# A state-space scan in two chunks of 256 tokens in place of four of 128, inside a fused Mamba-2 and LoRA kernel

## The reference

```python
A_cs = jnp.cumsum(A_dt, axis=-1)                      # within a chunk
Lmat = jnp.exp(segsum(A_dt))                          # exp(cs[l] - cs[s]), l >= s
M = einsum('bclhn,bcshn->bclsh', Cc, Bc) * Lmat       # C B^T times the decays
Y_diag = einsum('bclsh,bcshp->bclhp', M, X)           # inside a chunk
states = einsum('bclhn,bclhp->bchpn', Bc * exp(A_cs[-1] - A_cs), X)
new_states = einsum('bzjh,bzhpn->bjhpn', decay_chunk, states)   # recurrence over the chunks
Y_off = einsum('bclhn,bchpn->bclhp', Cc, prev_states) * exp(A_cs)
y = Y_diag + Y_off + D * hs
xg = y * silu(gate)                                   # then an RMS norm per group and out_proj
```

## Time and profile before

| | |
|---|---|
| median of 3 runs | 1766.87 us (1766.46 to 1768.51) |
| profiled execution | 1765.04 us, of which span 1763.3 us |
| busy: PE, DVE, ACT, POOL | 94%, 77%, 67%, 62% |
| share of the chain that ended last: PE, DVE, ACT | 72%, 17%, 5% |
| rows of the main loop | first L561 of batch 0 at 132 us, last L561 at 865 us; batch 1: 1009 and 1742 us |

### The profile page before, as it was taken

One profiled execution on the slowest core, in us unless ns is written; L12 is line 12 of the kernel. 1 busy time (PEld: TensorE's weight loads), 2 busy tenths in 40 slices (PEclk: granted clock), 3 DMA queues, 4 the chain that ended last, 5 costly groups with the idle time before them and its releaser, 6 DMA issues.

```text
span 1763.3 us, 28877 instructions
## 1 busy us (share of the span) xinstructions
PE 1666.0 (94%) x9694; PEld 1368.8 (78%) x9694; DVE 1354.8 (77%) x2398; ACT 1187.2 (67%) x2436; POOL 1084.6 (62%) x1358
## 2 busy tenths in 40 slices
PE   5889999999999999999868899999999999999997
PEld 4677878787878888788656778787878787887875
DVE  4877787877778787877668677878787878778785
ACT  2357777777777777777414577777777777777773
POOL 4236667666766667666543267666766676667764
PEclk9999999999999999999979899999999999999998
DMA  4144344334433344333132343344434443344431
GB/s 144 36 126 126 130 138 138 121 123 136 138 127 124 129 138 138 120 127 120 34 105 61 116 138 128 114 138 138 134 119 127 138 138 125 118 137 138 135 105 47
DMA packets 82434, 212.03 MB, mean 120 GB/s; under 512 B 11056, under 2 KB 27696, under 8 KB 82032
## 3 DMA queue, kind: packets, MB, share of 16 engines
q1 hardware_dynamic: 82288, 210.20, 36.8%
HBM read 207.01 MB, written 3.15 MB: 119 GB/s over the span
## 4 chain that ended last, share of the span: by engine, by line
PE 72%; DVE 17%; ACT 5%; issue 4%; DMA 1%; POOL 0%; SPq 0%; DVEq 0%; POOLq 0%; ACTq 0%
PE bh L454 20%; PE bg L454 17%; PE bo L593 15%; PE by L569 6%; DVE cv L618 5%; PE bt L561 4%; PE bt L580 4%; PE bt L600 2%; DVE acc L636 2%; ACT cv L258 2%; DVE mt L827 1%; DVE S L643 1%; DVE by L819 1%; PE bo L540 1%; PE bt L454 1%
## 5 line engine op out<-in xcount | busy, mean ns | idle before, releaser
L391 POOL TENSOR_TENSOR wl<-raw,wh 128x256 fp32r<-128x256 f32 x576 | 527.6, 947 | 146.1 <-ACT wh L254 146.1
L438 POOL TENSOR_TENSOR wol<-raw_o,woh 128x256 fp32r<-128x256 f32 x256 | 184.6, 743 | 483.0 <-ACT woh L358 483.0
L618 DVE SCALAR_TENSOR_TENSOR cv<-bh,par_sb,cv 128x511 f32<-128x511 f32 (+2 forms) x408 | 304.6, 747 | 191.0 <-ACT cv L258 185.8
L267 ACT ACTIVATE mt<-cs_row,cs_tok 128x128 f32<-128x128 f32 x1024 | 324.4, 389 | 0.0
L593 PE MATMUL bo<-woh,xh 128*128 128x512 f32 x512 | 212.7, 415 | 2.8 <-POOL xl L426 2.8
L593 PE MATMUL bo<-woh,xl 128*128 128x512 f32 x512 | 201.7, 394 | 0.0
L593 PE MATMUL bo<-wol,xh 128*128 128x512 f32 x512 | 199.9, 390 | 0.0
L325 ACT ACTIVATE xh<-xg 128x512 fp32r<-128x512 f32 x128 | 81.0, 633 | 166.1 <-DVE xg L823 166.1
L263 ACT ACTIVATE bh<-cv 128x512 f32<-128x512 f32 x136 | 81.8, 601 | 160.5 <-DVE cv L618 160.5
L426 POOL TENSOR_TENSOR xl<-xg,xh 128x256 fp32r<-128x256 f32 x256 | 182.6, 734 | 9.9 <-ACT xh L325 9.9
L811 DVE SCALAR_TENSOR_TENSOR sg<-tg,bg 128x512 f32<-128x512 f32 x128 | 87.9, 687 | 124.9 <-ACT tg L354 124.9
(11 more groups left out here) (168 smaller groups left out, 3354.5 us busy)
## 6 DMA issues: line engine op xcount, KB each, us to landing
raw<-in_w_step SPq DMA_DIRECT2D x128, 512.0 KB, 3.6
cs_row<-cs_rows SPq DMA_DIRECT2D x128, 512.0 KB, 4.3
raw_o<-in_w_out SPq DMA_DIRECT2D x128, 256.0 KB, 2.7
ec_row<-ec_rows SPq DMA_DIRECT2D x256, 96.0 KB, 3.7
raw<-in_w_bc SPq DMA_DIRECT2D x16, 512.0 KB, 4.1
acc<-in_x SPq DMA_DIRECT2D x2, 1024.0 KB, 8.6
mt<-in_w_ffn SPq DMA_DIRECT2D x2, 1024.0 KB, 7.6
out_dram<-acc SPq DMA_DIRECT2D x2, 1024.0 KB, 4.9
```

Of the source, the lines that this page charges most:

```text
L267: e = act.activation(mt[:, m % 2, h, chunk(j)], cs_row[:, m % 2, h, chunk(j)], ACT.Relu, bias=cs_tok[:, b, j, 2 * m + h:2 * m + h + 1], sc ...
L391: e = pool.tensor_tensor(wl[:, n % 2, part], raw[:, n % 2, part], wh[:, n % 2, part].bitcast(F32), ALU.subtract)
L438: e = pool.tensor_tensor(wol[:, 1 - u, part], raw_o[:, 1 - u, part], woh[:, 1 - u, part].bitcast(F32), ALU.subtract)
L618: dve.scalar_tensor_tensor(out=cv[:, u, k:], in0=src[:, 0:L - k], scalar=par_sb[:, un % UNITS, TAPS - 1 - k:TAPS - k], in1=cv[:, u, k:], o ...
```

## The change

The scan's chunk becomes 256 tokens (`CL`), so a batch has two chunks (`NC`). Of each chunk's 256x256 triangle three blocks of 128x128 are kept, as a row of 256 columns and one of 128 (`TRI` = 384 columns), for both chunks 768 in place of 512. Part by part, in a round of the main loop:

- line 267: the rows of blocks 0 and 2 get 256 columns, those of blocks 1 and 3 stay 128; `mt` has 1536 columns in place of 1024, so have the exp and the product with `gt`;
- state products: two, added up in PSUM, in place of three; the products inside a chunk: 8 as before, 4 of them with 256 columns; the carried product: one of 256 columns in place of three of 128, which waits for ScalarE's copy of the state and no longer for VectorE's recurrence;
- `next_state` (4 VectorE instructions) is gone; `xd`, `yo` and `by` plus `yo` have 256 columns in place of 384; each of the two `ec_row` DMAs brings 256 columns in place of 384.

In the group loop the B-C product has 256, 128, 256, 128 columns and two PSUM banks; the mask is applied in two instructions of 384 columns in place of one of 512; B is transposed for two blocks in place of three; the tables are made in rounds 4, 5 and 6, with one buffer in place of one per batch, and `cd_bc` is gone. In the prologue the cumulative sum is two instructions of 256 columns, the decay to the chunk's end one of 256 in place of three of 128. The core of the diff:

```diff
-NS = NJ - 1
+CL = 2 * P
+NC = L // CL
+TRI = CL + P
+        def span(j):
+            return slice(P * j, CL * (j // 2) + CL)
+        def tri(j):
+            return slice(TRI * (j // 2) + CL * (j % 2), TRI * (j // 2) + (CL if j % 2 == 0 else TRI))
...
                 for j in range(NJ):
-                    e = act.activation(mt[:, m % 2, h, chunk(j)], cs_row[:, m % 2, h, chunk(j)], ACT.Relu,
-                                       bias=cs_tok[:, b, j, 2 * m + h:2 * m + h + 1], scale=-1.0)
+                    e = act.activation(mt[:, m % 2, h, tri(j)], cs_row[:, m % 2, h, span(j)], ACT.Relu,
+                                       bias=cs_tok[:, j, 2 * m + h:2 * m + h + 1], scale=-1.0)
...
                         for j in range(NJ):
-                            mm = pe.matmul(bo[2][:, chunk(j)], h2[:, u, chunk(j)], ct[:, g - 1, chunk(j)],
-                                           start=True, stop=True)
+                            mm = pe.matmul(bo[2 + j // 2][:, CL * (j % 2):CL * (j % 2) + (P if j % 2 else CL)],
+                                           h2[:, u, chunk(j)], ct[:, g - 1, span(j)], start=True, stop=True)
...
-                        for c in range(NS):
-                            mm = pe.matmul(bt[:, chunk(c)], btok[:, g, c, :], xd[:, c, :], start=True, stop=True)
+                        for c in range(2):
+                            mm = pe.matmul(bt[:, 0:P], btok[:, g, c, :], xd[:, c, :], start=(c == 0), stop=(c == 1))
...
-                                mm = pe.matmul(by[HD * h:HD * (h + 1), chunk(j)], xt[:, j, HD * h:HD * (h + 1)],
-                                               mt[:, 1 - u, h, chunk(j)], start=True, stop=True)
+                                mm = pe.matmul(by[HD * h:HD * (h + 1), span(j)], xt[:, j, HD * h:HD * (h + 1)],
+                                               mt[:, 1 - u, h, tri(j)], start=(j % 2 == 0), stop=(j % 2 == 1),
+                                               skip_group_check=True)
...
-                        pe.wait_ge(v_s, did(n - 1, 4))
-                        for c in range(NS):
-                            mm = pe.matmul(bt[:, chunk(c)], S[:, c, :], ct[:, g, chunk(c + 1)], start=True, stop=True)
-                        mm.then_inc(t_off, 1)
+                        pe.wait_ge(a_s1, did(n - 1))
+                        pe.matmul(bt[:, CL:], S[:, :], ct[:, g, CL:], start=True, stop=True).then_inc(t_off, 1)
...
-            def next_state(b, i, c):
-
-                for h in range(2):
-                    cols = slice(HD * h, HD * (h + 1))
-                    dve.scalar_tensor_tensor(out=S[:, c, cols], in0=S[:, c - 1, cols],
...
-                    if has(m - 1):
-                        dve.wait_ge(a_s1, did(n - 1))
-                        next_state(b, m - 1, 1)
                     if has(m):
                         tap(un, u, bh, 2)
                         tap(un, u, bh, 3)
                     if has(m - 1):
-                        dve.wait_ge(v_s, did(n - 1, 4, 2))
-                        next_state(b, m - 1, 2)
                         dve.wait_ge(t_d, did(n - 1))
...
-                        dve.tensor_tensor(yo[:, :], bt[:, 0:NS * P], ec_row[:, 1 - u, :], ALU.mult).then_inc(v_off, 1)
+                        dve.tensor_tensor(yo[:, :], bt[:, CL:], ec_row[:, 1 - u, :], ALU.mult).then_inc(v_off, 1)
...
-                        dve.tensor_tensor(by[:, P:], by[:, P:], yo[:, :], ALU.add).then_inc(v_add, 1)
+                        dve.tensor_tensor(by[:, CL:], by[:, CL:], yo[:, :], ALU.add).then_inc(v_add, 1)
...
                         dve.tensor_tensor(mt[:, u], mt[:, u],
-                                          gt[:, m % GROUPS, :].unsqueeze(1).broadcast_to([P, 2, L]),
+                                          gt[:, m % GROUPS, :].unsqueeze(1).broadcast_to([P, 2, NC * TRI]),
                                           ALU.mult).then_inc(v_m, 1)
```

More of the change, by code:

```diff
@@ L369, in _ @@
             pool.memset(minus_half[:, :], -0.5).then_inc(const_ok, 1)
-            pool.memset(chunked[:, :], 1.0).then_inc(const_ok, 1)
-            pool.wait_ge(const_ok, 5)
+            pool.wait_ge(const_ok, 4)
             pool.affine_select(out=ident[:, :], in_=ident[:, :], compare_op=ALU.not_equal, fill=1.0, base=0,
                                pattern=[[-1, P]], channel_multiplier=1)
-            pool.affine_select(out=causal[:, :], in_=causal[:, :], compare_op=ALU.is_ge, fill=0.0, base=0,
-                               pattern=[[1, P]], channel_multiplier=-1)
-            pool.memset(chunked[:, :].rearrange("p (j c) -> p j c", j=NJ)[:, :, 0:1], 0.0).then_inc(const_ok, 1)
+            for own in (slice(0, P), slice(CL, TRI)):
+                e = pool.affine_select(out=causal[:, own], in_=causal[:, own], compare_op=ALU.is_ge, fill=0.0, base=0,
+                                       pattern=[[1, P]], channel_multiplier=-1)
+            e.then_inc(const_ok, 1)
             def scale_consts():
@@ L519, in _ @@
                     if g == 4:
-                        for dst, src in ((bo[0], csT), (bo[1], dtT)):
-                            for j in range(NJ):
-                                mm = pe.transpose(dst[:, chunk(j)], src[:, chunk(j)], ident[:, :])
+                        for j in range(NJ):
+                            mm = pe.transpose(bo[0][:, chunk(j)], csT[:, chunk(j)], ident[:, :])
                         mm.then_inc(pe_, 1)
@@ L525, in _ @@
                         pe.wait_ge(pa, b * PRO_ACT + ACT_TAB)
-                        for c in range(NS):
-                            pe.transpose(bo[0][:, chunk(c)], dtd[:, chunk(c)], ident[:, :])
-                        for c in range(1, NS):
-                            mm = pe.matmul(bo[1][:, chunk(c - 1)],
-                                           ecT[:, P * c + P - 1:P * c + P].broadcast_to([P, P]),
-                                           ident[:, :], start=True, stop=True)
+                        for j in range(NJ):
+                            mm = pe.transpose(bo[0][:, chunk(j)], dtT[:, chunk(j)], ident[:, :])
+                        mm.then_inc(pe_, 1)
+                    if g == 6:
+                        pe.wait_ge(pa, b * PRO_ACT + ACT_DTT)
+                        for c in range(2):
+                            mm = pe.transpose(bo[0][:, chunk(c)], dtd[:, chunk(c)], ident[:, :])
                         mm.then_inc(pe_, 1)
@@ L714, in prologue @@
                 link(dve.tensor_scalar(dh, dw, nA[:, 1:2], None, ALU.mult))
-                link(dve.tensor_tensor_scan(csT, chunked[:, :], dh, 0.0, ALU.mult, ALU.add))
+                for c in range(NC):
+                    part = slice(CL * c, CL * (c + 1))
+                    link(dve.tensor_tensor_scan(csT[:, part], ones[:, 0:1].broadcast_to([P, CL]), dh[:, part], 0.0,
+                                               ALU.mult, ALU.add))
                 assert done[0] == PRO_DVE_CS
```

96 lines of the change are left out of this document (45 added, 51 removed).

## The result

The changed kernel takes 1785.97 us (median of 4 runs, 1785.5 to 1786.63) against 1766.66 us of the kernel before (4 runs, 1766.29 to 1768.51): a ratio of 1.0107, 95% interval 1.009 to 1.0125. It is slower by 19.3 us. The direction was forecast, and the time lies inside the range of 1760 to 1787; the size wasn't, since the forecast was +7 us. The profiled execution took 1785.5 us (span 1783.8), 20.5 us more than that of before.

What follows compares the result with a forecast made beforehand. TensorE's own round and the ScalarE-VectorE chain were both taken to limit; +1.0 (groups with long rounds), +2.0 (rounds outside), +0.5 (batch ends) and +5.2 (group loop) made +8.7, say +8 us: 1774 us, range 1760 to 1787.

Steps and rivals of the forecast that it cites:

- What bounds the kernel: Main loop: X and P both limit; a pair of ordinary rounds costs X + P + 0.08, 22.68 us before, 22.97 forecast.
- X: Chain through ScalarE and VectorE to `xt`, from a round begun on time: 11.32 us before, forecast 11.63, bounds 11.51 and 11.72.
- P: TensorE's own work in a main-loop round: 11.28 us before, forecast 11.26 by the columns, bounds -0.15 and +0.21.
- the recurrence: `next_state` on VectorE between first and second tap, removed from X: -0.33 us; the second one gives nothing in ordinary rounds.
- the mask product: VectorE's `mt` times `gt` on 512 more columns, in X: +0.48 to +0.69 us, taken as +0.60.
- 4 pieces of 0.95 us: GpSimd's `wl` beside `mt` times `gt`: said to cover the longer instruction too, the reason for taking +0.60.
- The long rounds: Two rounds every eighth step: with the sum of squares 12.66 to 12.33 us, with `add_group` 12.69 to 12.2.
- The group loop: Its rounds go from 6.69 to 7.0 us, +3.0 per batch; with tables and cumulative sum +5.2 us in all.
- (a): TensorE's products inside the chunks: the two heads no longer run side by side, 0.21 us per round, 1788 us; chance 0.12.
- (b): VectorE's `mt` times `gt` costs only its columns, +0.48 in X, 1768 us, no change; chance 0.18.
- (c): Main loop: the scan's chain stops limiting, X falls under P, 1749 us, faster; chance 0.10.
- (d): The group loop hides its part: the sum without its 5.2 us, 1769 us; chance 0.15.

Runs made afterwards that it cites:

- e6: Changed kernel with the products inside the chunks at 128 columns each, the block below the diagonal left out of `y`: 1759.15 us, ratio 0.9971.
- e1: Kernel before with GpSimd making `wl` in 2 pieces of 512 columns in place of 4 of 256: 1789.65 us, ratio 1.0136.
- e2: Changed kernel with the product of `mt` and `gt` on 1024 of its 1536 columns: 1754.87 us, ratio 0.9941.
- e10: Kernel before with ScalarE's exp moved behind tanh, `woh` and `tg`, GpSimd not made to wait: 1758.28 us, ratio 0.9947.
- e5: Kernel before without `next_state`, the chunks' states not carried on: 1751.22 us, ratio 0.9928.
- e3: Changed kernel with GpSimd waiting for the mask product to be done before it starts `wl`: 1760.72 us, ratio 0.9968.
- e9: Changed kernel with ScalarE's exp moved behind tanh, `woh` and `tg`, GpSimd not made to wait: 1738.29 us, ratio 0.9834.

## Why the prediction was right in direction and wrong in size

**What bounds the kernel.** Right, and tested by `e6`: a pair is X + P + 0.08.

**P.** Forecast 11.26; early rounds of 11.32 to 11.37 us are that and 0.08. The parts hold: state products 0.54 to 0.61 us (forecast 0.55), products inside the chunks 1.45 (1.44), for the carried one -0.22 was forecast, and from its start to the second product of the output projection it is 0.67 us (291.52 to 292.19) in place of 0.89 (1328.00 to 1328.89).

**X.** Forecast 11.63, measured 11.89. Term by term: `by` plus `yo`, `yo` and `xd` -0.36 as forecast; exp 1.47 us in place of 1.04, +0.43 as forecast; the recurrence gave -0.26, not -0.33 (tanh starts 3.36 us into the round in place of 3.62), for I read the last two taps as 0.72 apart, where their row gives 1.53 for both, or 0.78 each; the mask product +0.80, not +0.60. With the -0.03 for the earlier state products this is 11.32 + 0.58 = 11.90, to 0.01 the round measured. Both bounds of X, 11.51 and 11.72, lie under it.

**The failed step** is the mask product: "I take +0.60, nearer to the proportional end, because `wl` (4 pieces of 0.95 us) covers the longer instruction too". Neither end of my range held it. A product in proportion to its length would have taken 1.382 x 1.5 = 2.07 us, one that only adds its columns 1.86 (0.94 ns each) or 1.91 (1.04). The runs put in its place: duration = duration alone + (time left of GpSimd's piece - 0.13 us). Five cases of it:

| kernel | alone | left of the piece | waited | measured |
|---|---|---|---|---|
| before | 1.215 | 0.30 | 0.17 | 1.38 |
| `e1` | 1.212 | 0.86 | 0.72 | 1.93 |
| `e2` | 1.212 | 0.57 | 0.44 | 1.65 |
| `e10`, with `add_group` | 1.215 | 0.59 | 0.46 | 1.67 |
| changed | 1.746 | 0.57 | 0.44 | 2.18 |

What is left depends on where both stand, and the change moved both: the mask product starts 8.63 us into the round in place of 8.73, and the first piece of `wl` ends 9.20 into it in place of 9.03, for on ScalarE `woh`, which GpSimd's `wol` waits for, follows the longer exp (6.36 us into the round in place of 6.20). I had counted the exp's 0.43 us in X and not asked what else is queued behind it. X came 0.26 above the forecast, 0.20 of it from this term. The mean pair came 0.19 above it (23.16 against 22.97; the pair shown above 0.24, while the first round and the last two of a batch are shorter, 11.1 to 11.5), which is 9.3 us over 49 pairs.

The "4 pieces of 0.95 us" were a sign, too: in the kernel before `wl` took 3.80 us for four pieces, but that is a first piece of 0.73, a second of 1.72 that stood still behind the mask product, and two more. The mean hid that one engine was waiting for the other.

**The rule that was there.** The rows of before showed the shortest and the median of line 827 0.17 us apart. The Trainium skill, "SBUF — State Buffer", section "Who interferes with whom", has a VectorE instruction with two SBUF inputs contend with a GpSimd one that reads SBUF, the lock exclusive and held for the whole instruction, the other side blocked and not slowed. I set it aside because 167 ns is "less than one piece of `wl`". That was no argument: a wait for a piece in progress is less than a piece. All five cases agree with the rule, and so do the other waits counted above. By it I also said that the wait "doesn't grow with length"; this is right too, but I took it to stay the same, and nothing in the rule says so.

**The long rounds.** With the sum of squares 12.29 against a forecast of 12.33. With `add_group` 12.58 against 12.2, because the mask product took 1.33 us there before and takes 2.25 now: +0.92 where +0.60 was put in. Of the 14 x 0.38 = 5.3 us, 0.32 us a round are thus the same error in another place; the rest is `next_state`, put at 0.71 us, where `e5` gives 0.64 (its round fell by 0.25 while its mask product grew by 0.39).

**The group loop.** The one round I showed came as forecast (7.01 us). Its six rounds behind the first gained 1.35 us per batch, where the sum put in 2.6 for loop, tables and cumulative sum together: two of them, from 7.57 to 7.45 and from 7.47 to 7.46 us, didn't grow. This is some 2.5 us too much in the sum. I had read one of eight rounds.

**Luck.** That the time fell inside the range of 1760 to 1787 doesn't bear out the sum. With X at its upper bound, 11.72, the sum gives 49 x 0.09 + 14 x 0.09 = 5.7 us more, about 1780; the range went up to 1787 to take in most of rival (a), which didn't happen.

**The rivals.** (a), pairing lost, gave 1788, the nearest number, and is refuted by the 1.45 us and by `e6`: a time that fits doesn't show a mechanism. (b), the mask product at its columns, is what `e3` makes true by an edit of its own, and the time is then that of before with the same edit. (c), the chain off the limit, came about only when exp was moved, and is the case in which this change pays. (d) is half true: about 2.7 of the 5.2 us came.

**Open.** Of the 2.5 us ahead of the first state product 1.2 are the group loop's. Over the twelve profiles that product starts between 129.0 and 136.1 us, also where the code ahead of it is the same, so the rest can't be put down to the change. How the 0.13 us in the wait arise isn't settled; in `e9` 11 mask products whose recorded start is 2 to 5 ns behind that of a new piece went ahead of it, so the recorded starts don't tell to that precision who comes first. Why the rounds with the sum of squares got shorter in `e1` as well isn't worked out either.

## What to carry to other kernels

Where an instruction's shortest duration and its median differ, ask at once which engine it overlaps with and how much of that engine's instruction is left when it starts: the difference is a wait that moves with phase, and an edit that only shifts either side reprices it. When an instruction gets longer, follow everything that is queued behind it on its engine, not only the chain that you are adding up. And of two versions compare also what they do once the obstacle before both is gone: this change costs 19 us, nothing that could be measured, or saves 9 or 20, by where the exp and `wl` stand.

## What the runs showed of the hardware

- A VectorE product of two SBUF tiles and a GpSimd product of SBUF tiles exclude each other for whole instructions: 1.21 us alone became 1.38, 1.65, 1.67 or 1.93 by the part of the piece that was left (all 746 waits in these profiles are what was left less 0.12 to 0.14 us, for both lengths of the product), and a GpSimd piece of 0.73 us behind the product took 2.26 us. With the two kept apart GpSimd's pieces have a mean of 736 ns, in place of 1058 in the changed kernel, and the product varies by 6 ns.
- A product with one input in PSUM isn't touched: `xt` has one, runs beside `wl` in 124 of 128 rounds and has 671/674/681 ns over all 128 in the changed kernel, and in `e3`, where `xt` falls into `wl`, the four pieces together still take 2.80 us.
- On TensorE two heads on different output partitions keep running side by side when their products alternate between 256 and 128 columns: 16 instructions in 1.45 us.
- Making GpSimd's instructions longer to save some (`e1`: mean 1664 ns each, 288 in place of 576, 473 us in place of 528 busy) lost 22 us in all: here the length of one piece counted for more than the number of them.
